# The constant of the denominators moves into a column beside each turned block, and ScalarE writes it

## The reference, cut to what matters

```python
def feature_map(x, orf):
    proj = x @ orf.T / d_k ** 0.25
    norm = jnp.sum(x * x, axis=-1, keepdims=True) / (2.0 * math.sqrt(d_k))
    return (jnp.exp(proj - norm) + EPS) / math.sqrt(m)
...
q = feature_map(split(x @ Wq.T + bq), orf)
k = feature_map(split(x @ Wk.T + bk), orf)
v = split(x @ Wv.T + bv)
kv = jnp.einsum('nlm,nld->nmd', k, v)
ksum = jnp.sum(k, axis=1)
out = jnp.einsum('nlm,nmd->nld', q, concatenate([kv, ksum[..., None]], axis=-1))
out = out[..., :-1] / out[..., -1:]
...
x = layernorm(x + out @ Wo.T + bo);  x = layernorm(x + ffn(x))
```

## Time and profile before

| | |
|---|---|
| median of 3 runs | 1328.44 us (1326.99 to 1329.98) |
| the profiled execution | 1326.88 us |
| its span, first to last instruction | 1325.0 us |
| granted TensorE clock, mean | 0.993 of full |
| busy: PE / PEld / DVE / ACT / POOL | 96% / 73% / 73% / 53% / 39% |
| the chain that ended last | PE 82%, DVE 7%, ACT 3% |

### The profile page before, as it was taken

The page is one execution under the profiler, slowest core; times in us unless marked ns, Lnnn a source line. Parts: engine busy times, 40 slices in busy tenths (PEclk is TensorE's granted clock), DMA queues, the critical chain, the costliest instruction groups (busy, mean ns, idle before and its releaser), DMA issues.

```text
span 1325.0 us, 24976 instructions
## 1 busy us (share of the span) xinstructions
PE 1277.0 (96%) x8522; PEld 961.2 (73%) x8522; DVE 969.8 (73%) x1821; ACT 696.8 (53%) x1337; POOL 513.3 (39%) x1005
## 2 busy tenths in 40 slices
PE   6999999999999999999999999999999999999796
PEld 5766788677877678776787668876688667886565
DVE  5688865887668875788658787578865787658875
ACT  5466535574355743557336653466544664455543
POOL 1234443254333453335424344334443344432433
PEclk9999999999999999999999999999999999999998
DMA  6567404674146721467115761267503674046511
GB/s 210 136 150 191 125 32 109 167 183 101 52 106 163 198 65 57 124 156 195 60 57 128 193 166 48 69 147 203 140 32 87 169 193 102 32 118 144 134 49 47
DMA packets 94013, 160.34 MB, mean 121 GB/s; under 512 B 31168, under 2 KB 47680, under 8 KB 93376
## 3 DMA queue, kind: packets, MB, share of 16 engines
q1 hardware_dynamic: 67712, 139.51, 40.9%
q10 hardware_dynamic: 9792, 17.12, 3.5%
q0 software_dynamic: 16384, 2.13, 1.1%
HBM read 39.13 MB, written 16.78 MB: 42 GB/s over the span
## 4 chain that ended last, share of the span: by engine, by line
PE 82%; DVE 7%; ACT 3%; issue 3%; SPq 3%; DMA 2%; POOL 1%; ACTq 0%; DVEq 0%; POOLq 0%
PE ps L835 29%; PE ps L872 23%; PE ps L933 7%; PE ps L858 4%; PE ps L904 4%; PE ps L860 4%; PE ps L859 4%; PE ps L891 3%; PE ps L949 2%; DMA rows<-in_x_t 1%; ACT features L602 1%; SPq L453 1%; SPq L442 1%; DVE squares_turned L753 1%; DVE stacks L715 1%
## 5 line engine op out<-in xcount | busy, mean ns | idle before, releaser
L602 ACT ACTIVATE features<-ps 128x512 f32<-128x512 f32 x512 | 278.8, 601 | 271.4 <-PE ps L835 200.0
L508 POOL DMA_DIRECT2D stacks<-norm_rows x512 | 253.0, 502 | 413.1 <-DVE norm_rows L768 172.6
L835 PE MATMUL ps<-Wo_hi,stacks 128*128 128x512 f32 x512 | 171.6, 401 | 4.5 <-DVE stacks L715 4.1
L487 POOL TENSOR_SCALAR stats<-stats 128x1 f32<-128x1 f32 x128 | 37.0, 289 | 328.3 <-DVE stats L697 328.3
L710 DVE TENSOR_TENSOR den<-den,features 128x512 f32<-128x512 f32 x192 | 134.7, 701 | 13.5
L576 ACT ACTIVATE values_then_attention<-ps 128x512 f32<-128x512 f32 x64 | 38.3, 599 | 199.0 <-PE ps L860 196.4
L835 PE MATMUL ps<-W_ternary,stacks 128*128 128x512 f32 x512 | 129.7, 396 | 6.2 <-DVE stacks L818 6.2
L933 PE MATMUL ps<-features,kv_ksum 128*32 128x512 f32 x1024 | 123.1, 598 | 10.0 <-ACT features L602 7.1
L835 PE MATMUL ps<-orf_key_a,stacks 128*128 128x256 f32 x512 | 131.7, 288 | 0.7 <-DMA stacks<-norm_rows 0.7
L835 PE MATMUL ps<-orf_key_b,stacks 68*128 68x256 f32 x512 | 128.5, 283 | 0.0
L551 ACT ACTIVATE rows<-rows,stats 128x512 f32<-128x512 f32 x128 | 101.0, 812 | 44.1 <-POOL stats L491 43.0
(11 more groups left out here) (112 smaller groups left out, 2649.3 us busy)
## 6 DMA issues: line engine op xcount, KB each, us to landing
stacks<-unit_hi SPq DMA_DIRECT2D x384, 128.0 KB, 2.4
stacks<-unit_lo SPq DMA_DIRECT2D x256, 128.0 KB, 3.2
stacks<-unit_hi SPq DMA_DIRECT2D x64, 256.0 KB, 3.8
out<-rows ACTq DMA_DIRECT2D x64, 256.0 KB, 2.0
rows<-in_x_t SPq DMA_DIRECT2D x56, 256.0 KB, 3.5
stacks<-norm_rows POOLq DMA_DIRECT2D x512, 4.0 KB, 2.6
rows<-in_x SPq DMA_DIRECT2D x32, 256.0 KB, 3.7
features<-in_x SPq DMA_DIRECT2D x32, 256.0 KB, 4.4
```

The source lines that it names most:

```text
L508: pool.dma_start(slot[row:row + 1, c:c + L].rearrange("o (t c) -> o t c", c=DH), NN[DH * h:DH * (h + 1), u % 2, part, :].bitcast(F32)).the ...
L602: nc.scalar.activation(FE[:, n % 8, :, 0:M], ps[:, :].rearrange("p (a m) -> p a m", a=HG), ACT.Exp, scale=C_EXP).then_inc(a_exp.sem, 1)
L835: last = mm(out, a, b, start=(n == 0), stop=(n == len(terms) - 1))
```

## The change

The block transposes of the denominators go to a buffer of their own, `dens_turned`, in which each block of 32 columns is followed by 2 more, so that a block takes 34. ACT writes EPS times the sum of ksum into the first of the two, for all 16 blocks at once (128x16), and EPS times the sum of kv into `CC` (128x1). Both are in stage KVT, behind feature tile 3. DVE's multiplication in stage G 7 is gone. In GG the addition of the constant to one column (TENSOR_SCALAR, 128x16) becomes a sum over two neighbouring columns, the block's last and the constant's (TENSOR_REDUCE, 16 sums of 2). All 32 rows that a block is made from are the same, so any of its columns will do. DVE now waits in GG for ACT's two writes; ACT waits, before it writes, for its own sums and for DVE's reciprocals of the group before.

```diff
+        DT = sb("dens_turned", [P, 16 * (DH + 2)])
+        turned = DT[:, :].rearrange("p (a c) -> p a c", c=DH + 2)
...
+        a_c = Signal("eps_sums_ready", 2 * NG)
...
+                elif kind == "KVT":
+                    act.wait_ge(a_kc.sem, a_kc.nth(b, 3 * u + 3))
+                    act.wait_ge(v_dr.sem, v_dr.nth(b, 4 * u))
+                    nc.scalar.activation(turned[:, :, DH], RSUM[:, 2 * u + 1:2 * u + 2].broadcast_to([P, 16]), ACT.Copy,
+                                         scale=EPS).then_inc(a_c.sem, 1)
+                    nc.scalar.activation(CC[:, 2 * u:2 * u + 1], RSUM[:, 2 * u:2 * u + 1], ACT.Copy, scale=EPS).then_inc(a_c.sem, 1)
...
-                elif kind == "G" and at[1] == 7:
-                    dve.wait_ge(a_kc.sem, a_kc.nth(b, 3 * u + 3))
-                    nc.vector.tensor_scalar(CC[:, 2 * u:2 * u + 2], RSUM[:, 2 * u:2 * u + 2], EPS, None,
-                                            ALU.mult).then_inc(v_c.sem, 1)
                 elif kind == "GG":
-                    n, turned, den = 2 * (2 * g + h), DR[:, h, :], by_token[h]
+                    n, den = 2 * (2 * g + h), by_token[h]
                     dve.wait_ge(t_gg.sem, t_gg.nth(b, 2 * g + h + 1))
                     dve.wait_ge(v_a.sem, v_a.nth(b, 2 * g + h - 1))
-                    nc.vector.transpose(turned, DN[:, :]).then_inc(v_dt.sem, 1)
+                    nc.vector.transpose(turned[:, :, 0:DH], DN[:, :].rearrange("p (a c) -> p a c", c=DH)).then_inc(v_dt.sem, 1)
                     dve.wait_ge(v_dt.sem, v_dt.nth(b, 2 * g + h + 1))
-                    dve.wait_ge(v_c.sem, v_c.nth(b, g + 1))
-                    nc.vector.tensor_scalar(den, turned.rearrange("p (a c) -> p a c", c=DH)[:, :, 0], CC[:, 2 * g + 1:2 * g + 2],
-                                            None, ALU.add).then_inc(v_dr.sem, 1)
+                    dve.wait_ge(a_c.sem, a_c.nth(b, 2 * g + 2))
+                    nc.vector.reduce_sum(den, turned[:, :, DH - 1:DH + 1], axis=mybir.AxisListType.X).then_inc(v_dr.sem, 1)
```

More of the change, by code:

```diff
@@ L277, in attention_kernel @@
         v_ks = Signal("features_added", 7 * NG)
-        v_kvc, v_c = Signal("kv_ready", NG), Signal("eps_sums_ready", NG)
+        v_kvc = Signal("kv_ready", NG)
         v_dt, v_dr = Signal("den_turned", 2 * NG, 1), Signal("den_steps", 2 * 2 * NG)
```

## The result

The changed kernel takes 1322.33 us (median of 11 executions, 1319.08 to 1325.35), the kernel before 1329.53 us (11 executions, 1326.20 to 1334.08) on the same chip. The ratio is 0.9942 with an interval of 0.9924 to 0.9961: 0.58% faster, 7.2 us by the medians and 7.7 by the ratio, where I had forecast 3.9.

What follows compares the result with a forecast made beforehand. PE was taken as the bound, busy 1277.0 of 1325.0 us, so gain comes only from its 48 us idle. 4.17 + 0.05 - 0.3 = 3.9 us less than the median of the runs gives 1324.5 us, range 1322.0 to 1328.2.

Steps and rivals of the forecast that it cites:

- The holds, and that they reach PE: Main forecast, 70%: POOL's work holds the small TENSOR_SCALAR up to 3452 ns, idling PE before O 0; the change ends this.
- excess less 1.6 us: Unit 7: PE's idle time before O 0 is the instruction's time over 0.24 us, less 1.6 us of slack.
- what the change removes: PE's idle time before O 0 from unit 7's holds in entries 0, 2, 5 and 6: 4.17 us.
- the holds of unit 5: Five long instructions at GG 1, 0.57 to 1.27 us; no PE idle time ending with R 1 follows, so worth nothing.
- ACT's delay: ACT's two small writes delay S by 0.2 us; in unit 5 this reaches PE, a loss of 0.3 us.
- P's delay lies within GG 1's wait: Unit 5: P of the next entry is late too, but within the same wait of PE, so nothing was added.
- the forecast's own range: 1322.0 to 1325.8 us at 70%: below if four chains are held in full, above if ACT's delay is 0.7 us.
- The sum over two columns and the transposes: DVE: the sum takes 0.18 us against 0.24, gaining 0.05 us in entry 7; transposes with step 34 show no difference.
- The removed multiplication: DVE's L776 in stage G 7, done while DVE waits anyway: its removal is worth nothing.
- Held until POOL pauses: Unit 7: an instruction is held by chance of where it falls in POOL's work, then stays held until POOL pauses.
- hold passed to another instruction: Second rival, 24%: the gain is absent or eaten, as when L715, now earlier, is held; 1326 to 1328.5 us.
- Slower: Third rival, 6%: ACT's two instructions bound unit 5 if their delay passes 1.5 us; 1334.7 us at 2 us.

Runs made afterwards that it cites:

- e1: Changed kernel with the sum of two columns again a TENSOR_SCALAR everywhere, new layout and ACT's writes kept; 1328.29 us, ratio 1.0012 to the kernel before.
- e2: Kernel before with one more wait on POOL, so its additions in unit 7 start only after the first part of R 0; 1322.88 us, ratio 0.9972.
- e9: Changed kernel with the TENSOR_SCALAR back at GG 0 of unit 7, DVE waiting ahead of it until POOL comes to its additions; 1329.69 us, ratio 1.0018.
- e5: Kernel before with two more POOL additions behind the two of rows and bias in unit 7; 1327.76 us, ratio 0.9992.
- e6: Changed kernel with two more POOL additions behind the two of rows and bias in unit 7; 1325.11 us, ratio 0.9966 to the kernel before.
- e7: Changed kernel with the TENSOR_SCALAR back only at GG 0 of unit 7 (8 of 64); 1325.18 us, ratio 0.9984 to the kernel before.
- e8: Changed kernel with the TENSOR_SCALAR back only at GG 1 of unit 5 (8 of 64); 1322.71 us, ratio 0.9962 to the kernel before.
- e10: Changed kernel with the TENSOR_SCALAR back everywhere but GG 0 of unit 7 and GG 1 of unit 5 (48 of 64); 1321.50 us, ratio 0.9952.
- e4: Changed kernel with DVE writing both constants in stage G 7 in place of ACT; 1322.46 us, ratio 0.9948 to the kernel before.

## Why the prediction was right in kind and too small

**The holds, and that they reach PE: right.** In the changed kernel they are gone, with the instruction's kind put back they return (e1), with POOL's additions moved they are gone again (e2). The rule "excess less 1.6 us" held in every profile, up to 3.8 us of lateness (e9). Only in entry 4 of e5 and e6 is there idle time before O 0 (0.27 and 0.30 us) without such a hold; there L715 itself was held.

**The step that failed: what the change removes.** The sum of the prediction has one large term, the holds of unit 7 with 4.17 us, read from one profiled execution; it stood for all that the change takes away, with nothing for the holds of unit 5. In its place the timed executions show 6.6 us when the TENSOR_SCALAR is back everywhere (e1). Unit 7's eight make 3.5 us of it (e7) and unit 5's eight 1.0 (e8), within the scatter; the 48 elsewhere make none (e10). Some 2 us of the 6.6 have no place in that account. As each of these differences is uncertain by about 1 us (an estimate from a scatter of 2 us and twelve or fewer executions), they may be chance or a cost that only all of them together have; it stays open.

**The term itself: right on the mean, by luck.** Five profiles of the same kernel have 4.17, 3.89, 3.69, 2.53 and 6.91 us, with three to six entries held. Their mean is 4.2, but I had only the one, and the range should have let the gain go to 7 us as a usual case; my lower end of 1322.0 let it by only just. That the term varies so fits the scatter of single executions. It is 2.4 us for the kernel before, 1.8 for the changed kernel, and 1.4 for e9, where every entry but the last is held.

**What is still missing.** The five profiled executions of before average 1326.6 us and are 1.7 shorter than its timed ones, while those of the changed kernel are not shorter; more held entries in timed executions would do that, and so would chance, since single executions scatter by 2.4 us (standard deviation) and the mean of five by 1.1. Among the profiles some of the difference isn't the change at all: from 35 to 45 us, before the first instruction that differs (68 us), four of the five of before have a granted clock of 0.83 and 28 products of PE, where the other one, and four of the five of the changed kernel, have 1.00 and 34. In the first comparison some of the 7.2 us is scatter between sets too, since four later sets of the changed kernel have ratios of 0.9955 to 0.9965.

**ACT's delay: right in size, its way to PE only in part.** 0.20 us was forecast and is measured. In entry 3, where nothing covers it, it reaches PE as forecast, but before P of the next entry (0.20 us, from none) and not before GG 1 (0.32 us against 0.30). All seven entries have this 0.2 us before P, 1.4 us in all, where I had said that P's delay lies within GG 1's wait. GG 1's wait gives back a part: over the entries 0 to 6 and five profiles each, P and GG 1 together have 5.7 us in the kernel before and 6.7 in the changed one. That is 1.0 us more, not 0.3; but e4's one profile has 6.7 too, without ACT's writes, so the loss isn't told from chance. ACT's small rows are longer than I said (0.25 and 0.22 for 0.17 to 0.2 us) and overlap more. My price for a delay of 0.7 us was wrong as well: with the waits that I gave it comes to 2.2 us and not 2.9, and the time to 1326.5, above the 1325.8 that I named as the end of the forecast's own range.

**The sum over two columns and the transposes: right.** 0.198 us against 0.18 forecast; no change of the transposes; 0.05 us less before O 0 in entry 7 (0.26 to 0.21). The removed multiplication gave nothing that shows: e1 is without it and no faster than before.

**The mechanism's ends: wrong in words.** "Held until POOL pauses" fell with e5. That an instruction which starts among the transfers is held by chance is wrong too: one that begins up to 0.87 us ahead of the first addition is held, and one that begins earlier isn't (e2).

**The rivals.** In unit 7 of the changed kernel no hold passed to another instruction of DVE; where POOL's additions came later (e2) or were more (e6) one did, and PE waited 0.5 us more for it in entry 7 of e2 and 0.30 us in entry 4 of e6. Slower was far off: ACT's delay would have had to be 1.5 us.

## What to carry to other kernels

Look at the largest duration of a small instruction, not only at its mean: 64 instructions of 0.24 us with a maximum of 3.45 were the whole case. If such an instruction meets POOL's work, change its kind (a TENSOR_REDUCE was never held: 320 of the new one in five profiles take 205 ns at most) or move POOL's work away from it, which gave 0.28% for one wait; then look at what the moved work holds instead. And a delay that comes by chance of alignment must be sized over several profiles of the same kernel; one gives a draw from a wide distribution.

## What the runs showed of the hardware that I hadn't expected

A TENSOR_SCALAR can be held by an addition of POOL that hasn't begun by the profile. In the first profile it was held when it began 0.86 us ahead of the addition (465.74, 3.44 us) and not when it began 0.93 us ahead (625.91, 0.23 us). Over the five profiles of before the edge lies at 0.87 us, where some are held and some not; one in e5 began 0.85 us ahead and wasn't held. Why so far ahead, no run here shows.

A held instruction waits past several instructions of POOL, each of which begins before the one ahead has ended: one or two transfers and two additions in the 3.4 us holds. But it came in ahead of the third addition in e5.
